# A fourth buffer of probabilities, one buffer for b_2, and a new hand-written order of the steps of a batch

## The chip, the cores and the metric

The kernel runs on one core of a Trainium2 chip. The metric is the device time of one execution in microseconds (us), median of three runs. All data are float32; products that need more than one pass are built from a high and a low part.

## The reference

The input `x` has 16 batches of 512 tokens with 256 features. Two networks read the layer-normed input, and their product is added to `x`:

```python
xn = layernorm(x)
s = talk(xn)              # 16 heads of 16; 512 x 512 logits per head
g = silu(local(xn))       # two layers
out = x + s * g

# talk: rope on q and k, then
logits = einsum('bhij,gh->bgij', q k^T * scale, Wpre)
attn = einsum('bhij,gh->bgij', softmax(logits), Wpost)
out = (attn @ v) @ Wout.T + bout

# local, per layer: shift half of the features by one token,
# q k v = h @ wqkv (8 heads of 64), l2norm of q and k, rotary,
# softmax over a window of 128 tokens and the one before, x += o @ wo,
# layernorm, h @ w1 + b1 -> a, g;  x += (a * gelu(g)) @ w2 + b2
```

## The kernel before, in words

All weights but the four large ones of each layer stay in SBUF. `program()` lays out one list of steps for the whole run: `FIRST_ORDER` for batch 0, `ORDER` for batches 1 to 14, `LAST_ORDER` for batch 15. A step is a name with indices, such as `scores.13`. Each engine has a function for each step that it takes part in, and `Counts.run` calls these in the order of the list. So the list sets the order of each engine's queue by itself; between engines there are only semaphores. An engine that waits in a step holds back all that it has in later steps.

The steps of the talk network, per batch: `expand.c` (POOL, L1561 to L1571) multiplies q by the pre-mixing weights, `part.c` makes the high part (ACT, L1041) and the low part (POOL, L1575), for two tiles of queries at a time. `scores.n` (64 of them) is six matmuls (L759 to L761) into bank S0 or S1 (n even or odd), a row maximum on DVE (L1307), and the exponential on ACT (L1054) into `probs`, which has PB buffers. `mixers.m` (32) takes the reciprocals of the row sums (DVE, L1299) and scales the post-mixing weights (ACT, L1062). `mix.m` is 64 matmul records (L776) on two tiles, 2m and 2m+1, into banks M0 and M1; ACT empties M0 and DVE empties M1 (both L573). `values.c` and `project.t` follow for each eight and sixteen tiles, in M0.

The steps of the local network, per layer l: `qkv.l.t`; on DVE the rotation (L1330) and the squared norms (L1338, L1344), on POOL the power -1/2 (`qkv`, L1586); `join.l.t` adds on DVE (L1357) and scales k on POOL (L1593); `q_turn` and `k_turn` transpose (L835) into F3 and M1. `local_scores.l.u` (8), `weigh.l.u` (POOL, L1601), `p_turn.l.u`, `local_values.l.u` (into M1; DVE empties it, L1416), `out_proj.l.t` (into F3; DVE adds the input, L1430), `half_turn`, `shift_turn`, `h_scale`, `h_turn`, then `up.l.i`, `hide.l.i` and `down.l.t`. The gate of the previous batch is finished in the first third of the next one: `bound`, `sigmoid.t` (DVE reciprocal, L1510), `silu` (POOL, L1623), `gated` (POOL, L1628), `store`. They use `x_mid`, which the DVE part of `out_proj.0.0` overwrites, so that one waits for `gated_done`.

The waits that the change touches, in ACT's `scores`:

```python
before = (n - PB) // 2
if n >= PB:
    act.wait_ge(filled["M1"], now.fill(("mix", before), "M1"))
```

PE may start `scores.n` when ACT has emptied that S bank of tile n-2 and when `part` of n//2 is done. It may start a `mix` when M0 and M1 have been emptied of what they held.

Of the kernel before, what the change touches and what calls it, by code (L numbers as in the profile page):

```python
# [136 lines left out]
weigh.0.6 project.0 weigh.0.7 local_values.0.4 p_turn.0.5 mix.9 p_turn.0.6 local_values.0.5 part.12 scores.21
out_proj.0.2 expand.13 local_values.0.6 p_turn.0.7 scores.22 local_values.0.7 mixers.10 scores.23 out_proj.0.3 mix.10
half_turn.0 mixers.11 part.13 scores.24 expand.14 shift_turn.0 mix.11 scores.25 scores.26 mixers.12 values.2 part.14
h_scale.0 scores.27 mix.12 mixers.13 expand.15 h_turn.0 part.15 scores.28 scores.29 mix.13 expand.16 up.0.0 mixers.14  # L140
# [1597 lines left out]
```

## Time and profile before

| what | us |
|---|---|
| median of 3 runs | 5136.95 (5134.96 to 5141.85) |
| the profiled execution | 5127.82 |
| its span, first to last instruction | 5126.0 |
| PE busy in the span | 4968.1 (97%) |
| DVE busy | 3403.0 (66%) |
| ACT busy | 3111.0 (61%) |
| POOL busy | 2884.7 (56%) |

A busy time is the union of an engine's instructions. The profile lists for each group of instructions the count, the mean duration, and the idle time of the engine just before them with what ended it. PE is the matmul engine, POOL is GpSimd. The page's mean DMA rate is 64 GB/s.

### The profile page before, as it was taken

To read this page: it belongs to the slowest core of one execution; us is meant where nothing else is said; L and a number is where in the kernel's file an instruction comes from. 1 tells how busy PE (TensorE), PEld (TensorE's weight loads), DVE (VectorE), ACT (ScalarE), POOL (GpSimd) and SP (SyncE) were. 2 spreads that over 40 slices of the span, in tenths; PEclk is the share of its full clock that TensorE was granted. 3 is DMA by queue.
4 is the path that set the end of the run, shared out by engine and by line. 5 is a ranking of instruction groups with operands and counts; after the bars stand their busy time and mean duration, and the time that the engine had idled before them with its cause. 6 is when DMAs were issued, how large, how long until landed. Compare 5 with 4: busy or idle time off the path is not lost. (4 is left out here: it accounts for less than half of the span.)

```text
span 5126.0 us, 184535 instructions
## 1 busy us (share of the span) xinstructions
PE 4968.1 (97%) x76184; PEld 4078.3 (80%) x76184; DVE 3403.0 (66%) x8316; ACT 3111.0 (61%) x8075; POOL 2884.7 (56%) x2500
## 2 busy tenths in 40 slices
PE   6999999999999999999999999999999999999998
PEld 5787888878878788788787877878788788878887
DVE  6557676676766667666676666767667676676765
ACT  4566655666655666556665566565566655666655
POOL 4547555465655656555565555655546555465653
PEclk9999999999999999999999999999999999999999
DMA  2312112121111211112111111112112122121111
GB/s 85 119 51 86 46 74 75 42 69 70 54 74 46 74 58 54 74 46 78 54 54 74 66 62 50 64 64 74 54 61 71 46 74 71 45 70 63 57 62 30
DMA packets 61215, 325.84 MB, mean 64 GB/s; under 512 B 6368, under 2 KB 23776, under 8 KB 43488
## 3 DMA queue, kind: packets, MB, share of 16 engines
q1 hardware_dynamic: 49632, 297.26, 15.4%
q0 software_dynamic: 10752, 16.78, 1.7%
q8 instruction: 610, 9.99, 0.8%
q14 instruction: 221, 1.81, 0.1%
HBM read 288.33 MB, written 34.08 MB: 63 GB/s over the span
## 5 line engine op out<-in xcount | busy, mean ns | idle before, releaser
L1575 POOL TENSOR_TENSOR q_lo<-q_mix,q_hi 128x512 fp32r<-128x512 f32 x512 | 662.1, 1293 | 863.0 <-ACT q_hi L1041 862.7
L1054 ACT ACTIVATE probs<-bank_S,neg_max 128x512 f32<-128x512 f32 x1024 | 699.0, 684 | 725.2 <-DVE neg_max L1307 639.1
L759 PE MATMUL bank_S<-k_hi,q_lo 128*128 128x512 f32 x2048 | 879.4, 429 | 35.3 <-POOL q_lo L1575 21.6
L1307 DVE TENSOR_REDUCE neg_max<-bank_S 128x1 f32<-128x512 f32 x1024 | 697.0, 687 | 295.8 <-PE bank_S L761 290.7
L761 PE MATMUL bank_S<-k_hi,q_hi 128*128 128x512 f32 x2048 | 806.3, 394 | 0.0
L760 PE MATMUL bank_S<-k_lo,q_hi 128*128 128x512 f32 x2048 | 805.6, 393 | 0.0
L1570 POOL TENSOR_TENSOR q_mix<-q_rope,w_pre 128x256 f32<-128x256 f32 x1024 | 633.1, 646 | 43.4 <-POOL q_lo L1575 0.9
L776 PEld LDWEIGHTS bank_M<-mixer_n,probs 64*64 64x64 f32 x32768 | 530.5, 135 | 155.9 <-issue 135.8
L776 PE MATMUL bank_M<-mixer_n,probs 64*64 64x64 f32 x32768 | 597.9, 221 | 8.1 <-DVE o_locT_lo L1416 3.4
L1601 POOL TENSOR_TENSOR l_probs<-l_probs,l_inv 128x1024 f32<-128x1024 f32 (+1 forms) x256 | 430.2, 1688 | 273.6 <-DVE l_inv L1410 272.8
L1586 POOL TENSOR_TENSOR inv_norms<-norms_c,minus_half 128x16 f32<-128x16 f32 x128 | 418.1, 3266 | 251.2 <-DVE norms_c L1344 249.2
L1607 POOL TENSOR_TENSOR hidden_lo<-shared,hidden_hi 128x512 fp32r<-128x512 f32 x192 | 246.5, 1300 | 547.0 <-ACT hidden_hi L1185 546.9
L1116 ACT ACTIVATE l_probs<-l_probs,l_least 128x256 f32<-128x256 f32 (+1 forms) x1024 | 480.2, 471 | 104.3 <-DVE l_least L1390 101.9
L759 PEld LDWEIGHTS bank_S<-k_hi,q_lo 128*128 128x128 f32 x2048 | 386.0, 188 | 170.2 <-issue 73.0
L573 DVE COPY mixed<-bank_M 128x512 f32<-128x512 f32 x512 | 352.0, 687 | 190.8 <-PE bank_M L776 187.1
L1041 ACT ACTIVATE q_hi<-q_mix 128x512 fp32r<-128x512 f32 x512 | 321.0, 627 | 250.5 <-POOL q_mix L1570 248.8
L761 PEld LDWEIGHTS bank_S<-k_hi,q_hi 128*128 128x128 f32 x2048 | 386.1, 189 | 89.6 <-issue 0.3
L760 PEld LDWEIGHTS bank_S<-k_lo,q_hi 128*128 128x128 f32 x2048 | 388.1, 190 | 56.0
L1390 DVE CUSTOM_DVE_ANT_0 l_probs<-bank_F,mask,inv_norms 128x256 f32<-128x256 f32 (+1 forms) x1024 | 403.5, 448 | 0.7 <-issue 0.7
L1062 ACT ACTIVATE mixer_n<-mixer,row_inv 128x64 f32<-128x64 f32 x1024 | 300.8, 344 | 112.8 <-DVE row_inv L1299 111.9
L1487 DVE SCALAR_TENSOR_TENSOR shared<-bank_F,b,shared 128x512 f32<-128x512 f32 x192 | 143.6, 748 | 327.7 <-ACT shared L1179 308.0
L1330 DVE TENSOR_TENSOR shared<-bank_F,rot 128x512 f32<-128x512 f32 x512 | 323.6, 684 | 51.9 <-PE bank_F L709 51.2
(157 smaller groups left out, 11372.0 us busy)
## 6 DMA issues: line engine op xcount, KB each, us to landing
w_qkv_hi<-split_qkv SPq DMA_DIRECT2D x30, 1536.0 KB, 9.7
w_qkv_lo<-split_qkv SPq DMA_DIRECT2D x30, 1536.0 KB, 6.4
w_hi<-split SPq DMA_DIRECT2D x30, 1408.0 KB, 6.1
w_lo<-split SPq DMA_DIRECT2D x30, 1408.0 KB, 6.1
w_hi<-split SPq DMA_DIRECT2D x30, 768.0 KB, 5.4
w_lo<-split SPq DMA_DIRECT2D x30, 768.0 KB, 7.2
w_o_hi<-split_o SPq DMA_DIRECT2D x30, 512.0 KB, 3.7
w_o_lo<-split_o SPq DMA_DIRECT2D x30, 512.0 KB, 4.7
```

The lines of the kernel that those rows point to most:

```text
L759: mm(bank[k][:], q_lo[q], k_hi[:, s, :], start=(s == 0), stop=False)
L760: mm(bank[k][:], q_hi[q], k_lo[:, s, :], start=False, stop=False)
L761: last = mm(bank[k][:], q_hi[q], k_hi[:, s, :], start=False, stop=(s == 1))
L776: last = mm(bank[f"M{r}"][keys, at:at + GH * HI], probs[rows, (2 * m + t) % PB, j * P + keys.start:j * P + keys.stop], mixer_n[rows, m % 2 ...
L1054: fn(probs[:, n % PB, :], bank[k][:], ACT.Exp, bias=neg_max[:, n % 2:n % 2 + 1], accum_out=row_sum[:, n % 4:n % 4 + 1]).then_inc(emptied[k ...
L1116: fn(l_probs[:, u % LB, j, lo:], l_probs[:, u % LB, j, lo:], ACT.Exp, scale=-1.0, bias=l_least[:, u % 2, j:j + 1], accum_out=l_sum[:, u % ...
L1307: v.tensor_reduce(neg_max[:, n % 2:n % 2 + 1], bank[k][:], AX.X, ALU.max, negate=True)\
L1390: ins = v.tensor_tensor_reduce(l_probs[:, u % LB, j, lo:], bank[k][:, pair * 2 * P + lo:(pair + 1) * 2 * P], mask[:, lo:], inv_norms[:, t, ...
L1570: g.tensor_tensor(q_mix[:, s].rearrange("p m (i g) -> p (m i) g", g=GH), q[:, :, None].to_broadcast(shape), w_pre[:, None, :].to_broadcast ...
L1575: g.tensor_tensor(q_lo[:, c % QB], q_mix[:], q_hi[:, c % QB].bitcast(F32), ALU.subtract)\
L1586: g.tensor_tensor(inv_norms[:, t, :], norms_c[:], minus_half[:], ALU.pow).then_inc(inv_norm_done, 1)
L1601: g.tensor_tensor(l_probs[:, u % LB, :, lo:], l_probs[:, u % LB, :, lo:], l_inv[:, u % 2, :, None].to_broadcast([P, 4, 2 * P - lo]), ALU.m ...
```

## The change

`PB` goes from 3 to 4, so the exponential of tile n waits for `mix` of (n-4)//2 and not of (n-3)//2. `b_2`, which had one buffer for each layer, filled once, has one for both; it is loaded by a DMA on SP's queue at each `out_proj.l.0`, after a wait for the last use, and POOL waits for it in `half_turn`. `ORDER` is new throughout; the other two orders stay. Of `ORDER` the diff below shows the stretches that are spoken of.

```diff
--- before
+++ after
@@ -28,7 +28,7 @@
 CI = CT * RI
 CHUNKS = TILES // CT
 PAIRS = TILES // 2
-PB = 3
+PB = 4
 GR = 4
 RH = 2
 HI = RI // RH
...
 ORDER = """
-expand.0 part.0 expand.1 qkv.0.0 join.0.0 part.1 scores.0 scores.1 qkv.0.1 scores.2 expand.2 bound q_turn.0.0 mixers.0
-join.0.1 part.2 k_turn.0.0 expand.3 qkv.0.2 q_turn.0.1 k_turn.0.1 scores.3 scores.4 part.3 mix.0 join.0.2 mixers.1
-expand.4 qkv.0.3 part.4 q_turn.0.2 mix.1 scores.5 join.0.3 mixers.2 k_turn.0.2 scores.6 scores.7 expand.5 mix.2
-sigmoid.0 part.5 expand.6 q_turn.0.3 k_turn.0.3 mixers.3 scores.8 part.6 local_scores.0.0 scores.9 mix.3
...
-weigh.0.1 mix.4 weigh.0.2 mixers.5 scores.12 sigmoid.2 expand.8 local_values.0.0 part.8 p_turn.0.1 expand.9 scores.13
-silu mix.5 sigmoid.3 gated p_turn.0.2 local_values.0.1 mixers.6 part.9 local_scores.0.3 scores.14 scores.15
-out_proj.0.0 mix.6 store expand.10 mixers.7 local_scores.0.4 weigh.0.3 scores.16 scores.17 part.10 mix.7 expand.11
...
-up.0.1 hide.0.0 hide.0.1 up.0.2 part.16 up.0.3 hide.0.2 hide.0.3 up.0.4 up.0.5 hide.0.5 hide.0.4 scores.30 expand.17
-mix.14 scores.31 scores.32 mixers.15 down.0.0 down.0.1 down.0.2 down.0.3 part.17 expand.18 part.18 mix.15 x_turn.1
-expand.19 scores.33 qkv.1.0 join.1.0 part.19 qkv.1.1 join.1.1 values.3 q_turn.1.0 k_turn.1.0 qkv.1.2 mixers.16
-q_turn.1.1 k_turn.1.1 scores.34 join.1.2 scores.35 expand.20 mix.16 part.20 qkv.1.3 k_turn.1.2 q_turn.1.2 mixers.17
-scores.36 join.1.3 scores.37 mix.17 q_turn.1.3 scores.38 k_turn.1.3 expand.21 part.21 mixers.18 project.1
...
-local_values.1.7 mixers.26 project.2 expand.29 out_proj.1.3 part.29 expand.30 scores.54 half_turn.1 scores.55 mix.26
-mixers.27 part.30 scores.56 expand.31 shift_turn.1 mix.27 scores.57 scores.58 mixers.28 h_scale.1 values.6 part.31
-scores.59 mix.28 mixers.29 h_turn.1 scores.60 scores.61 mix.29 mixers.30 up.1.0 up.1.1 hide.1.0 scores.62 norm
-hide.1.1 scores.63 mix.30 mixers.31 up.1.2 up.1.3 mix.31 scale hide.1.2 hide.1.3 up.1.4 values.7 x_turn.0 up.1.5
-project.3 hide.1.5 hide.1.4 talk_k talk_q down.1.0 down.1.1 down.1.2 talk_v down.1.3
+expand.0 part.0 expand.1 qkv.0.0 part.1 join.0.0 scores.0 expand.2 scores.1 qkv.0.1 mixers.0 k_turn.0.0 part.2
+join.0.1 q_turn.0.0 scores.2 expand.3 qkv.0.2 part.3 q_turn.0.1 expand.4 k_turn.0.1 scores.3 bound scores.4 join.0.2
+part.4 expand.5 mix.0 qkv.0.3 mixers.1 k_turn.0.2 scores.5 join.0.3 part.5 q_turn.0.2 scores.6 expand.6 mix.1 mixers.2
+scores.7 k_turn.0.3 sigmoid.0 part.6 scores.8 mixers.3 mix.2 expand.7 scores.9 q_turn.0.3 part.7 sigmoid.1 scores.10
+mix.3 mixers.4 local_scores.0.0 scores.11 expand.8 weigh.0.0 values.0 part.8 local_scores.0.1 mixers.5 mix.4
+local_scores.0.2 scores.13 scores.12 p_turn.0.0 weigh.0.1 weigh.0.2 local_scores.0.3 mix.5 scores.14 scores.15
+expand.9 sigmoid.2 local_values.0.0 part.9 mixers.6 mixers.7 p_turn.0.1 expand.10 scores.16 scores.17 mix.6
+local_scores.0.4 sigmoid.3 local_values.0.1 silu weigh.0.3 p_turn.0.2 gated part.10 expand.11 scores.18 scores.19
+mix.7 mixers.8 local_scores.0.5 out_proj.0.0 local_values.0.2 weigh.0.4 values.1 mixers.9 p_turn.0.3 local_scores.0.6
+mix.8 scores.20 scores.21 p_turn.0.4 store weigh.0.5 weigh.0.6 local_values.0.3 part.11 mixers.10 local_scores.0.7
...
+scores.24 mix.10 out_proj.0.3 mix.11 half_turn.0 scores.25 part.14 shift_turn.0 scores.26 expand.15 scores.27 part.15
+values.2 mixers.12 h_scale.0 expand.16 mixers.13 scores.28 scores.29 mix.12 h_turn.0 scores.30 mix.13 mixers.14
+scores.31 mixers.15 up.0.0 up.0.1 part.16 hide.0.0 hide.0.1 mix.14 up.0.2 up.0.3 hide.0.2 hide.0.3 up.0.4 expand.17
+up.0.5 mix.15 hide.0.5 hide.0.4 scores.32 scores.33 values.3 mixers.16 down.0.0 down.0.1 down.0.2 part.17 expand.18
+part.18 expand.19 down.0.3 mix.16 part.19 x_turn.1 scores.34 expand.20 scores.35 part.20 qkv.1.0 mixers.17 join.1.0
+qkv.1.1 expand.21 mix.17 q_turn.1.0 scores.36 scores.37 join.1.1 k_turn.1.0 qkv.1.2 k_turn.1.1 mixers.18 part.21
+join.1.2 scores.38 expand.22 q_turn.1.1 qkv.1.3 mix.18 q_turn.1.2 scores.39 scores.40 join.1.3 part.22 expand.23
+k_turn.1.2 mixers.19 project.1 scores.41 q_turn.1.3 k_turn.1.3 mixers.20 part.23 expand.24 scores.42 local_scores.1.0
...
+p_turn.1.1 mixers.22 mixers.23 weigh.1.3 scores.48 scores.49 mix.22 local_scores.1.4 scores.50 mix.23 p_turn.1.2
...
+local_values.1.7 mixers.26 expand.30 scores.55 mixers.27 out_proj.1.3 mix.26 half_turn.1 mix.27 shift_turn.1 part.30
+scores.56 scores.57 values.6 h_scale.1 mixers.28 scores.58 scores.59 h_turn.1 mix.28 mixers.29 scores.60 scores.61
+norm expand.31 up.1.0 up.1.1 mix.29 hide.1.0 hide.1.1 scale up.1.2 part.31 mixers.30 hide.1.2 up.1.3 mix.30 x_turn.0
+scores.62 scores.63 hide.1.3 mixers.31 up.1.4 up.1.5 mix.31 talk_k hide.1.5 hide.1.4 talk_q values.7 talk_v down.1.0
+down.1.1 down.1.2 down.1.3 project.3
 """
...
         b_1 = [sb(f"b_1{l}", [BLOCKS]) for l in range(LAYERS)]
-        b_2 = [sb(f"b_2{l}", [D]) for l in range(LAYERS)]
+        b_2 = sb("b_2", [D])
...
         opener = sb("opener", [1])
@@ -461,6 +461,7 @@
         w_1_loaded = sem("w_1_loaded", 16 * LAYERS, -16 * LAYERS)
         w_1_lo_loaded = sem("w_1_lo_loaded", 16 * LAYERS, -16 * LAYERS)
         w_2_loaded = sem("w_2_loaded", 32 * LAYERS, -32 * LAYERS)
+        b_2_loaded = sem("b_2_loaded", 16 * LAYERS)
         o_hi_done = sem("o_hi_done", TW * QUADS * LAYERS)
         hidden_hi_done = sem("hidden_hi_done", LAYERS * HC)
         hidden_lo_done = sem("hidden_lo_done", LAYERS * HC)
@@ -515,7 +516,7 @@
         for l in range(LAYERS):
             once += [
                 (scales[l], a["scales"][l]), (b_1[l][:], a["b_1"][l]),
-                (b_2[l][:], a["b_2"][l]), (ln_w[l][:], a["ln_w"][l]),
+                (ln_w[l][:], a["ln_w"][l]),
             ]
         LOADED = 16 * len(once)
         TABLES = 2 + 4 * LAYERS + 2
@@ -641,8 +642,12 @@
                         sp.dma_start(w_1_lo[:].bitcast(F32), split_1[l, 1]).then_inc(w_1_lo_loaded, 16)
 
             def out_proj(step, l, t):
-                if t == 0 and now.first:
-                    spill_o(l)
+                if t == 0:
+                    if now.first:
+                        spill_o(l)
+                    if now.past(l):
+                        sp.wait_ge(mid_b_ready, now.at(mid_b_ready, l))
+                    sp.dma_start(b_2[:], a["b_2"][l]).then_inc(b_2_loaded, 16)
                 if t == TW - 1:
                     sp.wait_ge(filled["F3"], now.fill(step, "F3"))
                     sp.wait_ge(o_spilled, 32 * (l + 1) if now.first else 32 * LAYERS)
@@ -710,6 +715,8 @@
 
             def x_turn(step, l):
                 stream_ready(pe, now, l)
+                if now.b == 1 and not l:
+                    pe.wait_ge(bias_folded, LAYERS)
                 for c in range(KC):
                     if now.was_filled(step, f"F{c}"):
                         pe.wait_ge(emptied[f"F{c}"], now.fill(step, f"F{c}") - 1)
@@ -1609,7 +1616,8 @@
 
             def half_turn(step, l):
                 pool.wait_ge(emptied["F3"], now.fill(("out_proj", l, TW - 1), "F3"))
-                g.tensor_tensor(x_mid_b, x_mid[:], b_2[l][:, None, :].to_broadcast([P, TW, D]), ALU.add)\
+                pool.wait_ge(b_2_loaded, now.at(b_2_loaded, 16 * (l + 1)))
+                g.tensor_tensor(x_mid_b, x_mid[:], b_2[:, None, :].to_broadcast([P, TW, D]), ALU.add)\
                     .then_inc(mid_b_ready, 1)
                 if not l and now.b < B - 1:
```

## Rows read from the trace of the kernel before

**Rows 1.** The page: engines, busy us, share of the span, instructions.
```profile
PE 4968.1 (97%) x76184; PEld 4078.3 (80%) x76184; DVE 3403.0 (66%) x8316; ACT 3111.0 (61%) x8075; POOL 2884.7 (56%) x2500
```

**Rows 2.** The page: busy tenths of PE in 40 slices of the span.
```profile
PE   6999999999999999999999999999999999999998
```

**Rows 3.** Busy by stretch (batches 1 to 14): us, engines with counts, clock, DMA.
```profile
397.30:4800.60 4403.30, 4321.29 (x66585) 3546.26 (x66586) 2955.97 (x7254) 2707.35 (x7056) 2520.33 (x2187) 1.00 0.18 62
```

**Rows 4.** Waits of PE, batches 1 to 14: us in total, times, longest.
```profile
PE bank_M L835 <- POOL shared L1593: 16.8, 28, 1.0
PE bank_S L759 <- POOL q_lo L1575: 16.2, 14, 1.2
PE bank_S L759 <- ACT probs L1054: 12.9, 14, 0.9
PE bank_M L795 <- issue: 10.5, 14, 1.5
PE bank_M L835 <- DVE mixed L573: 5.8, 14, 0.4
PE bank_F L707 <- DVE xT_lo L1263: 4.6, 14, 0.6
PE bank_F L718 <- DVE shared L1487: 3.4, 13, 0.4
PE bank_M L776 <- DVE o_locT_lo L1416: 3.4, 14, 0.2
```

**Rows 5.** PE in order of time, batch 6, around scores.31 and scores.32: start, duration.
```profile
2104.40 0.40 PE L760 MATMUL bank_S<-k_lo,q_hi 128*128 128x512 f32 x1
2104.63 0.40 PE L761 MATMUL bank_S<-k_hi,q_hi 128*128 128x512 f32 x1
2105.95 0.47 PE L759 MATMUL bank_S<-k_hi,q_lo 128*128 128x512 f32 x1 [0.92 <-ACT probs L1054]
```

**Rows 6.** POOL in order of time, the start of batch 6 (qkv.0.0 starts at 1966.26).
```profile
1972.19 3.92 POOL L1586 TENSOR_TENSOR inv_norms<-norms_c,minus_half 128x16 f32<-128x16 f32 x1 [2.25 <-DVE norms_c L1344]
1976.18 1.05 POOL L1593 TENSOR_TENSOR shared<-shared,inv_norms 128x512 f32<-128x512 f32 x1
1977.19 1.27 POOL L1575 TENSOR_TENSOR q_lo<-q_mix,q_hi 128x512 fp32r<-128x512 f32 x1
1979.02 2.90 POOL L1586 TENSOR_TENSOR inv_norms<-norms_c,minus_half 128x16 f32<-128x16 f32 x1 [0.57 <-DVE norms_c L1344]
```

**Rows 7.** DVE in order of time, the same stretch: the addition of join.0.0.
```profile
1972.11 1.23 DVE L1357 TENSOR_TENSOR shared<-shared 128x1024 f32<-128x1024 f32 x1
```

**Rows 8.** PE in order of time, batch 6: mix.10, half_turn.0, scores.24.
```profile
2066.99 1.16 PE L776 MATMUL bank_M<-mixer_n,probs 64*64 64x64 f32 x64
2068.09 0.66 PE L911 MATMUL bank_F<-ident,x_mid 128*128 128x128 f32 x4
2068.50 0.48 PE L759 MATMUL bank_S<-k_hi,q_lo 128*128 128x512 f32 x1
```

**Rows 9.** DVE in order of time: it empties M1 of mix.10.
```profile
2068.32 0.69 DVE L573 COPY mixed<-bank_M 128x512 f32<-128x512 f32 x1 [0.79 <-PE bank_M L776]
```

**Rows 10.** Groups by line, DVE, shapes apart, batch 6: busy, mean ns, idle before.
```profile
L1307 DVE TENSOR_REDUCE neg_max<-bank_S 128x1 f32<-128x512 f32 x64 | 43.5, 687 | 19.9 <-PE bank_S L761 19.6
L1390 DVE CUSTOM_DVE_ANT_0 l_probs<-bank_F,mask,inv_norms 128x256 f32<-128x256 f32 x48 | 20.5, 481 | 0.0
L1510 DVE RECIPROCAL x_mid<-x_mid 128x256 f32<-128x256 f32 x4 | 7.0, 1739 | 0.0
```

**Rows 11.** Groups by line, POOL, shapes apart, batch 6.
```profile
L1601 POOL TENSOR_TENSOR l_probs<-l_probs,l_inv 128x1024 f32<-128x1024 f32 x12 | 22.7, 1898 | 9.9 <-DVE l_inv L1410 9.8
L1623 POOL TENSOR_TENSOR x_mid<-x_mid,x_tok 128x1024 f32<-128x1024 f32 x1 | 2.4, 2412 | 0.7 <-DVE x_mid L1510 0.7
L1628 POOL TENSOR_TENSOR s_tok<-s_tok,x_mid 128x1024 f32<-128x1024 f32 x1 | 2.4, 2397 | 0.1
```

**Rows 12.** DMA issues by line: engine, count, KB each, median us to landing.
```profile
b<-in_b SPq DMA_DIRECT2D x2, 128.0 KB, 4.0
```

More of the change, by code:

```diff
@@ L126 @@
 ORDER = """
-expand.0 part.0 expand.1 qkv.0.0 join.0.0 part.1 scores.0 scores.1 qkv.0.1 scores.2 expand.2 bound q_turn.0.0 mixers.0
-join.0.1 part.2 k_turn.0.0 expand.3 qkv.0.2 q_turn.0.1 k_turn.0.1 scores.3 scores.4 part.3 mix.0 join.0.2 mixers.1
-expand.4 qkv.0.3 part.4 q_turn.0.2 mix.1 scores.5 join.0.3 mixers.2 k_turn.0.2 scores.6 scores.7 expand.5 mix.2
-sigmoid.0 part.5 expand.6 q_turn.0.3 k_turn.0.3 mixers.3 scores.8 part.6 local_scores.0.0 scores.9 mix.3
-local_scores.0.1 weigh.0.0 scores.10 expand.7 mixers.4 values.0 sigmoid.1 part.7 local_scores.0.2 scores.11 p_turn.0.0
@@ L132 @@
-weigh.0.1 mix.4 weigh.0.2 mixers.5 scores.12 sigmoid.2 expand.8 local_values.0.0 part.8 p_turn.0.1 expand.9 scores.13
-silu mix.5 sigmoid.3 gated p_turn.0.2 local_values.0.1 mixers.6 part.9 local_scores.0.3 scores.14 scores.15
-out_proj.0.0 mix.6 store expand.10 mixers.7 local_scores.0.4 weigh.0.3 scores.16 scores.17 part.10 mix.7 expand.11
-local_scores.0.5 scores.18 weigh.0.4 weigh.0.5 p_turn.0.3 local_values.0.2 mixers.8 values.1 local_scores.0.6
-local_values.0.3 p_turn.0.4 part.11 scores.19 scores.20 mix.8 mixers.9 local_scores.0.7 out_proj.0.1 expand.12
@@ L137 @@
[L137 to L140, printed above, removed]
-up.0.1 hide.0.0 hide.0.1 up.0.2 part.16 up.0.3 hide.0.2 hide.0.3 up.0.4 up.0.5 hide.0.5 hide.0.4 scores.30 expand.17
@@ L147 @@
-part.22 mix.19 local_scores.1.2 scores.42 weigh.1.1 weigh.1.2 local_values.1.0 values.4 mixers.20 expand.23
-local_scores.1.3 p_turn.1.1 scores.43 mix.20 scores.44 local_values.1.1 part.23 mixers.21 weigh.1.3 p_turn.1.2
-scores.45 local_scores.1.4 expand.24 mix.21 part.24 mixers.22 scores.46 expand.25 weigh.1.4 out_proj.1.0
-local_values.1.2 p_turn.1.3 part.25 scores.47 mix.22 mixers.23 local_scores.1.5 scores.48 scores.49 mix.23
-local_scores.1.6 weigh.1.5 p_turn.1.4 local_values.1.3 expand.26 mixers.24 values.5 part.26 expand.27 local_scores.1.7
@@ L152 @@
-scores.50 out_proj.1.1 weigh.1.6 mix.24 p_turn.1.5 weigh.1.7 local_values.1.4 scores.51 local_values.1.5 part.27
-p_turn.1.6 mixers.25 scores.52 expand.28 out_proj.1.2 local_values.1.6 p_turn.1.7 part.28 mix.25 scores.53
-local_values.1.7 mixers.26 project.2 expand.29 out_proj.1.3 part.29 expand.30 scores.54 half_turn.1 scores.55 mix.26
-mixers.27 part.30 scores.56 expand.31 shift_turn.1 mix.27 scores.57 scores.58 mixers.28 h_scale.1 values.6 part.31
-scores.59 mix.28 mixers.29 h_turn.1 scores.60 scores.61 mix.29 mixers.30 up.1.0 up.1.1 hide.1.0 scores.62 norm
@@ new lines @@
+mix.7 mixers.8 local_scores.0.5 out_proj.0.0 local_values.0.2 weigh.0.4 values.1 mixers.9 p_turn.0.3 local_scores.0.6
+mix.8 scores.20 scores.21 p_turn.0.4 store weigh.0.5 weigh.0.6 local_values.0.3 part.11 mixers.10 local_scores.0.7
+project.0 out_proj.0.1 local_values.0.4 p_turn.0.5 expand.12 mix.9 p_turn.0.6 local_values.0.5 weigh.0.7 part.12
+scores.22 out_proj.0.2 expand.13 local_values.0.6 p_turn.0.7 scores.23 local_values.0.7 part.13 mixers.11 expand.14
+scores.24 mix.10 out_proj.0.3 mix.11 half_turn.0 scores.25 part.14 shift_turn.0 scores.26 expand.15 scores.27 part.15
@@ new lines @@
+join.1.2 scores.38 expand.22 q_turn.1.1 qkv.1.3 mix.18 q_turn.1.2 scores.39 scores.40 join.1.3 part.22 expand.23
+k_turn.1.2 mixers.19 project.1 scores.41 q_turn.1.3 k_turn.1.3 mixers.20 part.23 expand.24 scores.42 local_scores.1.0
+mix.19 scores.43 local_scores.1.1 values.4 weigh.1.0 part.24 local_scores.1.2 mixers.21 mix.20 scores.45 scores.44
+weigh.1.1 p_turn.1.0 local_scores.1.3 weigh.1.2 mix.21 expand.25 scores.46 scores.47 local_values.1.0 part.25
+p_turn.1.1 mixers.22 mixers.23 weigh.1.3 scores.48 scores.49 mix.22 local_scores.1.4 scores.50 mix.23 p_turn.1.2
@@ new lines @@
+weigh.1.4 local_values.1.1 local_scores.1.5 expand.26 scores.51 out_proj.1.0 weigh.1.5 local_values.1.2 p_turn.1.3
+part.26 mixers.24 values.5 local_values.1.3 p_turn.1.4 mix.24 mixers.25 expand.27 part.27 local_scores.1.6 weigh.1.6
+out_proj.1.1 project.2 local_values.1.4 expand.28 p_turn.1.5 part.28 mix.25 local_scores.1.7 expand.29
+local_values.1.5 p_turn.1.6 weigh.1.7 scores.52 scores.53 out_proj.1.2 part.29 local_values.1.6 p_turn.1.7 scores.54
+local_values.1.7 mixers.26 expand.30 scores.55 mixers.27 out_proj.1.3 mix.26 half_turn.1 mix.27 shift_turn.1 part.30
```

1 line of the change is left out of this document (removed).

## The prediction

> **What bounds the kernel now.** First the page: PE is busy for 97% of the span [rows 1], and in the 40 slices only the first is clearly short [rows 2]. So the only things worth asking are how much PE stands idle, and at which steps. Then the busy table: in batches 1 to 14, all of which run `ORDER`, PE is busy 4321.29 of 4403.30 us [rows 3]. That is 314.5 us a batch with 82.0 / 14 = 5.9 us idle, at a granted clock of 1.00, so no step there pays for a low clock. DVE, ACT and POOL are busy 67%, 61% and 57% of it; they set the end only where PE waits for them. Then the waits of PE [rows 4]: nearly all come 14 or 28 times, with nearly the same length, so they are places in the order and not chance. The change touches no matmul's size or number; it can move only these waits, bring new ones, and change what neighbours what.
>
> A wait costs more than its idle time. scores.32 starts 2105.95 - 2104.63 = 1.32 us after the last matmul of scores.31, where 0.23 is the usual distance, so the 0.92 idle cost 1.09 [rows 5]. I add 0.17 to each wait.
>
> **Waits that go**, per batch:
> - scores.32 waits for ACT to empty S0 (12.9 / 14 = 0.92) [rows 4]. Before, the exponential of scores.30 stands in ACT's queue behind all of up.0 and hide.0. In the new order tiles 28 to 31 are exponentiated ahead of up.0.0, and mix.14 and mix.15 run among the `up` steps; that needs the fourth buffer. Late next is S0 for scores.34, with 14 us of values.3 and down.0 in between. 1.09.
> - k_turn.1.0 and k_turn.1.1 wait for POOL's scaling of k (16.8 / 14 = 1.20 in two waits). Now mix.17 and two scores, some 4 us, stand between qkv.1.1 and k_turn.1.0, and all of qkv.1.2 (4.2 us) before k_turn.1.1. My addition of POOL's work there (power 3.9, expand.21 1.2, join 1.0) has it ready at 169.2 us from the batch's start where PE comes at 169.4. 1.20 + 0.34 = 1.54.
> - k_turn.0.3 waits for DVE to empty M1 after mix.2 (5.8 / 14 = 0.41); now it comes ahead of mix.2. 0.58.
> - qkv.1.0 waits for the low part of x (0.33); two scores instead of one cover it. 0.50.
> - x_turn.0 waits for DVE in F0 and F1 (3.4 / 13 = 0.26); it now follows mix.30. 0.43.
> - mix.5 waits for M1, because local_values.0.0 came just ahead (0.24). Now that comes after. 0.41.
>
> Sum 4.55 us a batch.
>
> **A wait that only moves.** scores.2 waits 1.16 for part.1, which POOL runs behind the power of qkv.0.0 and join.0.0 [rows 4]. The power starts at 1972.19, 5.93 after the batch's start, when DVE has the norms; then 3.92, 1.05 and 1.27 us follow, and part.1 is done at 12.2 [rows 6]. The new order swaps part.1 and join.0.0 and puts k_turn.0.0, which needs join.0.0, ahead of scores.2. The same three instructions end at 12.2 and PE arrives at 11.1 either way. Zero; a gain of 1.0 if the swap shortened it, a loss of 1.0 if expand.2, now ahead of the power of qkv.0.1, pushes join.0.2 (I have 27.0 for it against PE's 27.7) and join.0.3 (33.4 against 33.9) over their edge.
>
> In these rows the power takes 3.92 when it starts beside DVE's addition of two SBUF tiles, and 2.90 later [rows 6, 7]. The Trainium skill, SBUF — State Buffer, section SBUF: two separate sides, says that GpSimd and a DVE operation with two SBUF inputs exclude each other on a shared port for a whole instruction, and whichever starts first holds it. That agrees with POOL's 1.02 lost here; the other half, DVE held up by a running POOL instruction, these rows do not show. By that rule DVE's join.0.1 would stand behind a running power, and k_turn.0.1 with it; the sum would be 21 to 41 us higher, as worked out from rows in the second rival.
>
> **Waits that come**, per batch:
> - mix.27 has only half_turn.1 between it and mix.26. A mix starts at 2066.99, DVE copies M1 from 2068.32 for 0.69, so M1 is free 2.02 after the start [rows 8, 9]. Mix and half_turn take 1.10 + 0.41 = 1.51 on PE [rows 8]. 0.5, and a little for the restart: 0.55. The pair mix.10 and mix.11 has out_proj.0.3 (1.5) between and is clear.
> - scores.58 needs S0, whose maximum stands on DVE behind shift_turn.1 (3.0). My addition has it 0.3 late. 0.3.
> - The knot of sigmoid.3, silu, gated and out_proj.0.0. DVE: local_scores.0.4 (four of 0.48 and small ones, 2.05), sigmoid.3 1.74 [rows 10]; POOL: silu 2.41, weigh.0.3 1.90, gated 2.40 [rows 11]; DVE: out_proj.0.0 0.42, which waits for `gated_done`. With 0.1 a hop, 11.3 us. PE's cover from the end of local_scores.0.4 to the F3 half of p_turn.0.3 is 11.1. Behind the waiting out_proj.0.0 stand DVE's local_values.0.2, weigh.0.4 and local_scores.0.6. Before it, DVE runs behind PE: between scores.12 and scores.17 stand six maxima of 0.69 and sigmoid.2 [rows 10], and local_values.0.1 and mix.7 each find M1 some 0.1 to 0.2 late. 0.8 in all; from 0 (DVE in time) to 3.9 (a rival).
> - About ten other places where my addition leaves under 0.3 us: part.10 before scores.20, weigh.1.7 before p_turn.1.7, the exponential of scores.26, M1 before mix.10 and local_values.1.1. From 0 to 2.5; I take 0.8, a third, as before such places cost mostly nothing.
>
> Sum 2.45 us a batch.
>
> **Edits at no cost.** Scores follow scores 21 times instead of 15, and mixes come after scores 11 times instead of 20; setting the distances of PE's step starts in the trace against both sequences gives 304.0 us a batch without waits for the old and 304.1 for the new, so zero, with 0.6 either way. The waits called issue at `values` (10.5 / 14 = 0.75) [rows 4] have no engine behind them and stay. b_2: one more DMA of 128 KB a layer, 4.0 us to landing [rows 12], issued at out_proj.l.0 some 30 us ahead of half_turn; what SP waits for is a layer old, and the load behind it is due only at local_values.l.7. With no cover it would be 4.0 x 2 = 8 us a batch, on POOL, and only partly on PE. Two loads fewer before the start: 0 to 1 us, taken 0. Batches 0 and 15 keep their orders and gain only looser exponentials: 0 to 2 us, taken 1.
>
> **The sum.** 4.55 - 2.45 = 2.1 us a batch, 29 us in 14, 30 in all. The profiled execution took 5127.8 with a span of 5126.0; 5098 for its like. The median lies 9.1 above the profiled one, so 5107 as a median.
>
> **Rivals.**
> - *Deeper gain* (5065): the new places are all in time and most waits found are gone: 4.55 and the 1.3 of part.1 with it, (4.55 + 0.5) x 14 = 71. For it: three of the four engines are a third idle. Against: mix.27's copy cannot be in time.
> - *The wait moves, nothing is won* (5137): POOL and DVE are late at other steps by as much, 4.5 a batch, because my additions leave no room for contention. One such mechanism: DVE's join.0.1, due while POOL runs the power of qkv.0.1 (2.90 [rows 6]), is held back by it for half of it or all, 1.5 to 2.9 us a batch, which alone turns 5107 into 5128 to 5148. The rows so far show only POOL giving way. (The Trainium skill, SBUF — State Buffer, section SBUF: two separate sides, has both sides giving way.)
> - *The knot closes* (5155, slower): one mechanism. sigmoid.3, silu and gated hold DVE at out_proj.0.0 and PE at p_turn.0.3. It costs one for one beyond 11.1 us; it cancels the gain from 2.1 us more than I have, and with DVE 3.5 late the price is (3.5 - 2.1) x 14 = 19 above 5137. For: DVE's queue is full there. Against: it is 67% busy over the batch and DVE catches up at every PE step without work for it.
> - *The change doesn't bite*: with b_2's load late, half_turn would wait. 30 us of cover against 4: 2 in 100.
>
> **Numbers.** Near the forecast 0.45, deeper gain 0.22, nothing won 0.17, knot 0.13, other 0.03. About 0.2% (10 us) is what a measurement of this kernel can tell from no change. Faster by more: 0.43 + 0.22 + 0.05 of the third case = 0.70; within: 0.13; slower: 0.17. Range 5060 to 5148; around the likeliest alone 5088 to 5125.
>
> **What would show it.** In the waits of PE after: L759 on ACT probs (12.9) and L835 on DVE mixed gone; L835 on POOL shared still at 14 to 18, now once a batch at k_turn.0.0, and L759 on POOL q_lo near nothing; a new row L776 on DVE mixed of 4 to 8; DVE idle before L1430 on POOL s_tok. Batches 1 to 14 at 312.4 us each, idle 3.5 to 4.5. It is wrong if PE's idle is unchanged, or if idle falls and the batch doesn't.

## The result: 0.24% slower

The changed kernel takes 5148.05 us (median; 5137.79 to 5157.77) and the kernel before, run beside it on the same chip, 5134.96 (5127.53 to 5141.85). The ratio is 1.0024, 95% interval 1.0016 to 1.0032. The forecast was 5107, faster; the range's upper end, 5148, is just missed by the median, and the sign is wrong. The profiled executions are a little apart from their medians (before 5127.8, after 5154.1), so differences between these two traces come to 26 us where the medians differ by 13.

### The profile page after: what moved, and what is told of

Same layout as the page of the kernel before. It is cut to its first block and busy times, and to the rows that moved or that the text cites. A ratio compares the mean times of both kernels' runs of the same rounds, so it can differ in the third digit from the quotient of the medians.

```text
span 5152.0 us, 184596 instructions
## 1 busy us (share of the span) xinstructions
PE 4962.2 (96%) x76184; PEld 4108.2 (80%) x76184; DVE 3415.7 (66%) x8316; ACT 3127.4 (61%) x8075; POOL 2878.2 (56%) x2500
## 3 DMA queue, kind: packets, MB, share of 16 engines
q8 instruction: 610, 9.99, 0.8%
## 5 line engine op out<-in xcount | busy, mean ns | idle before, releaser
L1582 POOL TENSOR_TENSOR q_lo<-q_mix,q_hi 128x512 fp32r<-128x512 f32 x512 | 672.7, 1314 | 748.5 <-ACT q_hi L1048 748.4
L766 PE MATMUL bank_S<-k_hi,q_lo 128*128 128x512 f32 x2048 | 875.0, 427 | 19.2 <-ACT probs L1061 11.1
L768 PE MATMUL bank_S<-k_hi,q_hi 128*128 128x512 f32 x2048 | 808.4, 395 | 0.0
L783 PEld LDWEIGHTS bank_M<-mixer_n,probs 64*64 64x64 f32 x32768 | 542.5, 135 | 170.2 <-issue 139.3
L1577 POOL TENSOR_TENSOR q_mix<-q_rope,w_pre 128x256 f32<-128x256 f32 x1024 | 621.2, 628 | 47.4 <-POOL q_lo L1582 0.9
L783 PE MATMUL bank_M<-mixer_n,probs 64*64 64x64 f32 x32768 | 604.7, 221 | 34.3 <-issue 24.5
L1593 POOL TENSOR_TENSOR inv_norms<-norms_c,minus_half 128x16 f32<-128x16 f32 x128 | 391.4, 3058 | 188.3 <-DVE norms_c L1351 184.6
L766 PEld LDWEIGHTS bank_S<-k_hi,q_lo 128*128 128x128 f32 x2048 | 388.2, 190 | 129.7 <-issue 54.3
L768 PEld LDWEIGHTS bank_S<-k_hi,q_hi 128*128 128x128 f32 x2048 | 387.7, 189 | 89.0
L1614 POOL TENSOR_TENSOR hidden_lo<-shared,hidden_hi 128x512 fp32r<-128x512 f32 x192 | 260.4, 1373 | 353.7 <-ACT hidden_hi L1192 353.7
L574 ACT COPY mixed<-bank_M 128x512 f32<-128x512 f32 x512 | 296.6, 579 | 181.0 <-PE bank_M L783 179.5
```

The source lines that it names most:

```text
L574: copy(to, bank[k][:].rearrange("p (t c i) -> p t c i", t=2, i=HI)).then_inc(emptied[k], 1)
L766: mm(bank[k][:], q_lo[q], k_hi[:, s, :], start=(s == 0), stop=False)
L768: last = mm(bank[k][:], q_hi[q], k_hi[:, s, :], start=False, stop=(s == 1))
L783: last = mm(bank[f"M{r}"][keys, at:at + GH * HI], probs[rows, (2 * m + t) % PB, j * P + keys.start:j * P + keys.stop], mixer_n[rows, m % 2 ...
L1577: g.tensor_tensor(q_mix[:, s].rearrange("p m (i g) -> p (m i) g", g=GH), q[:, :, None].to_broadcast(shape), w_pre[:, None, :].to_broadcast ...
L1582: g.tensor_tensor(q_lo[:, c % QB], q_mix[:], q_hi[:, c % QB].bitcast(F32), ALU.subtract)\
```

## The profile after

The span, PE's part of the page and its slices, then the busy table of batches 1 to 14 (the stretch of [rows 3]; columns as there). Lines of the new kernel stand 7 lower than the old ones: `scores` L766 to L768, `mix` L783, `values` L802, the turns of k L842, `local_values` L894.

```profile
span 5152.0 us, 184596 instructions
PE 4962.2 (96%) x76184; PEld 4108.2 (80%) x76184; DVE 3415.7 (66%) x8316; ACT 3127.4 (61%) x8075; POOL 2878.2 (56%) x2500
PE   6999999999999999999999999999999999999998
...
q8 instruction: 610, 9.99, 0.8%
```

```profile
399.27:4826.47 4427.20, 4311.74 (x66584) 3572.40 (x66585) 2970.90 (x7254) 2723.46 (x7057) 2514.47 (x2188) 1.00 0.18 63
```

A batch takes 316.2 us instead of 314.5 [rows 3], and PE stands idle for 115.5 us instead of 82.0. PE's waits in the same stretch, to be set against [rows 4]:

```profile
PE bank_M L783 <- issue: 23.9, 24, 2.4
PE bank_M L802 <- issue: 23.4, 22, 3.2
PE bank_M L842 <- POOL shared L1600: 17.4, 28, 1.1
PE bank_M L802 <- ACT mixed L574: 12.3, 14, 0.9
PE bank_S L766 <- ACT probs L1061: 10.5, 42, 0.4
PE bank_M L894 <- DVE mixed L574: 9.2, 28, 0.3
PE bank_M L783 <- DVE mixed L574: 5.8, 14, 0.4
PE bank_F L863 <- DVE l_least L1397: 3.5, 8, 0.5
PE bank_F L863 <- issue: 2.5, 3, 1.1
```

The engine waits changed places as meant. The two top rows are new in kind: 46 waits called issue (the profile found nothing that released them), up to 3.2 us long and not in every batch. Before, that name had 10.5 us at `values` [rows 4], a row at `local_scores` that [rows 4] leave out, and 0.2 us at `mix`:

```profile
PE bank_F L856 <- issue: 4.7, 15, 0.7
```

The longest one, in PE's timeline (start, duration, line and operation, in brackets the idle time before):

```profile
1454.31 0.90 PE L802 MATMUL bank_M<-mixed,v_heads 128*32 128x64 f32 x51
1458.45 0.48 PE L802 MATMUL bank_M<-mixed,v_heads 128*32 128x64 f32 x9 [3.24 <-issue]
1458.86 0.80 PE L766 MATMUL bank_S<-k_hi,q_lo 128*128 128x512 f32 x1
1459.45 0.63 PE L767 MATMUL bank_S<-k_lo,q_hi 128*128 128x512 f32 x1
```

PE stops in the middle of `values`, between two matmuls of one loop that read the same tiles; nothing can have become ready there but the instruction itself. Behind it the matmuls of scores take 0.63 us instead of 0.39. The table of windows has the reason (PE busy, PEld, DVE, ACT, POOL, granted clock, DMA share, GB/s):

```profile
1450.00:1458.40 8.40, 5.21 (x136) 4.15 (x135) 7.04 (x26) 3.38 (x8) 5.72 (x9) 1.00 0.51 197
1458.40:1461.90 3.50, 3.45 (x17) 2.66 (x17) 0.08 (x1) 1.33 (x5) 1.00 (x2) 0.52 0.02 5
1461.90:1470.00 8.10, 8.06 (x157) 6.36 (x156) 4.86 (x9) 4.03 (x10) 0.00 (x0) 1.00 0.01 3
```

After the wait TensorE runs for 3.4 us at the lower of its two clock levels (0.52 of 2.4 GHz, that is 1.2 GHz). That happens six times in batches 1 to 14, for 3.4 us five times and 6.8 us once, each time at an issue wait of 1.5 to 3.2 us; before, it never happens in these batches. Not every such wait does it: 11 waits are 1.5 us or longer, and behind two of 2.4 and 2.0 us, among others, the clock stays up. At half speed these 23.8 us cost up to 11.9 us beside the waits.

**What runs out.** In the table of DMA queues, between 1454 and 1459, one packet is an instruction block:

```profile
q0 software_dynamic: 27, 0.08, 4.1%
q1 hardware_dynamic: 6, 0.02, 1.4%
q8 instruction: 1, 0.02, 1.2%
```

Queue q8 has 610 packets and 9.99 MB in the whole run, 16 KB each; one holds 256 instructions, as experiment 3 shows. PE has 2 x 76184 records, 595 blocks. Then I took each issue wait above 0.4 us in batches 1 to 14 and counted PE's records, loads and matmuls together, up to it, adding 240 a batch for instructions that leave no record (2 x 76184 + 16 x 240 = 156,208 = 610.2 blocks, the number of packets; that 240 is my fit). Modulo 256 the 45 waits of the new kernel lie at 187 to 196, and the 18 of the old one at 186 to 192. So PE waits at the border of a block. At these waits a fetch takes 0.9 to 1.4 us of packet time, and the wait ends 1.2 to 1.6 us after the fetch has ended. The Trainium skill, Runtime: NRT & Kernel Launch, section Instruction fetch mechanics, says that each engine's instructions come in 16 KiB blocks of 256 by a DMA queue of its own, which agrees, and that crossing a border is mostly hidden because instructions are dispatched more slowly than they are fetched. This trace disagrees for PE: 3.24 us at one border.

`mix` uses up 128 instructions in 1.1 us and `values` 256 in 1.9 us, while `scores` takes 1.5 us over 12. At the two dense steps a block lasts 2 to 4 us with what lies about them. The new order puts dense steps nearer each other: from values.0 to local_scores.0.2 416 records in 4.1 us where nothing is fetched late, mix.26 and mix.27 with one turn between, mix.10 and mix.11 with one out_proj (they start 2.7 us apart). By step the issue waits are mix.27 7.0, mix.11 6.8, values.2 6.2, values.3 5.5, mix.4 4.5, mix.20 4.4, values.6 4.0, values.0 3.7, values.4 3.5; before, only `values` and `local_scores` have more than 0.3 us.

PE's time per batch, worked out for each trace from all its idle times (rest is what is not idle; "issue" is the profile's name, and experiment 8 shows that it can hide an engine):

| kernel | batch | issue | engines | rest |
|---|---|---|---|---|
| before | 314.52 | 1.22 | 4.66 | 308.63 |
| after | 316.23 | 4.01 | 4.27 | 307.95 |
| old order | 314.45 | 1.37 | 4.60 | 308.48 |
| b_2 once | 315.62 | 3.67 | 4.29 | 307.66 |
| shifted | 316.25 | 4.09 | 4.24 | 307.93 |
| spaced, seven edits | 314.55 | 3.04 | 3.30 | 308.21 |
| spaced, six edits (second run) | 314.36 | 3.30 | 2.73 | 308.33 |
| spaced more | 318.46 | 4.50 | 5.70 | 308.26 |
| six edits and mix.15 | 314.15 | 2.55 | 3.55 | 308.05 |

## The experiments

**1. Everything but the order.** The changed kernel with the `ORDER` of before.

```diff
-expand.0 part.0 expand.1 qkv.0.0 part.1 join.0.0 scores.0 expand.2 scores.1 qkv.0.1 ...
+expand.0 part.0 expand.1 qkv.0.0 join.0.0 part.1 scores.0 scores.1 qkv.0.1 scores.2 ...
```

> The changed kernel with the old ORDER: four buffers of probabilities and b_2 in one buffer loaded per layer stay, only the order of steps goes back. Theory A (the new order thins out PE's supply of instructions: it puts mix, values and mix closer together, and the waits called issue, 55 us in batches 1 to 14 after against 16 before, are waits for instructions): as the kernel before, 5130 to 5140, ratio 0.999 to 1.001, issue waits at mix and values back to 10 to 16 us, no fall of the clock in batches 1 to 14. Theory B (the 30 further loads of b_2, in packets of 1 KB, hold up the fetching of instructions): 5145 to 5155, ratio 1.002 to 1.004, issue waits of 40 us or more. Theory C (PB alone does something): any other time.

Measured: 5131.91 us, ratio 0.9997 [0.9988, 1.0006]. Issue waits are back:

```profile
PE bank_M L802 <- issue: 10.1, 17, 1.0
PE bank_F L863 <- issue: 4.5, 12, 1.0
...
PE bank_M L783 <- issue: 1.1, 4, 0.4
```

At `mix` and `values` they sum to 11 us, within the 10 to 16 expected, and the clock does not fall in batches 1 to 14. The order alone makes the kernel slower; the fourth buffer and b_2's loads cost nothing that can be measured.

**2. The new order, b_2 loaded in the first batch only** (layer 0 of the later batches then adds the bias of layer 1).

```diff
-                    if now.past(l):
-                        sp.wait_ge(mid_b_ready, now.at(mid_b_ready, l))
-                    sp.dma_start(b_2[:], a["b_2"][l]).then_inc(b_2_loaded, 16)
+                    if now.first:
+                        if now.past(l):
+                            sp.wait_ge(mid_b_ready, now.at(mid_b_ready, l))
+                        sp.dma_start(b_2[:], a["b_2"][l]).then_inc(b_2_loaded, 16)
...
-                pool.wait_ge(b_2_loaded, now.at(b_2_loaded, 16 * (l + 1)))
+                if now.first:
+                    pool.wait_ge(b_2_loaded, now.at(b_2_loaded, 16 * (l + 1)))
```

> The changed kernel, but b_2 is loaded in batch 0 alone; from batch 1 on both layers use the b_2 of layer 1, so 30 loads of 128 KB are left out and the bias of layer 0 is another one. Theory A (instruction supply, by the order): no change against the changed kernel, ratio to before 1.001 to 1.004, issue waits 40 to 70 us. Theory B (the loads of b_2): ratio 0.999 or lower, issue waits under 25 us.

Measured: 5148.81 us, ratio 1.0027 [1.0016, 1.0039], with the issue waits at the same steps:

```profile
PE bank_M L784 <- issue: 23.9, 22, 2.4
PE bank_M L803 <- issue: 18.0, 18, 1.9
```

b_2's loads do not hold the instruction blocks up. Whether other loads do was not tried. The trace of the changed kernel speaks for it in part: all seven waits of 2 us or more have 160 to 380 GB/s of other transfers from 4 us before the wait to its end, where the mean of the stretch is 63, and the packet of their block starts 0.4 us before PE stops at the earliest. But of the 22 waits of 0.4 us or more with under 5 GB/s around them the longest is still 1.7 us. One window of either kind:

```profile
650.80:657.20 6.40, 3.68 (x97) 3.13 (x97) 1.87 (x4) 3.05 (x9) 2.35 (x1) 0.92 0.94 377
4390.90:4396.70 5.80, 3.25 (x124) 2.44 (x123) 2.39 (x13) 4.52 (x21) 2.25 (x3) 1.00 0.01 3
```

**3 and 4. Half as many instructions in `mix`, in either order.** A mix's four 64x64 tiles become two of 64x128, so 32 matmuls and 32 loads instead of 64 and 64, with the same products. It is a slower mix: what counts is the two orders against each other.

```diff
-                            for half in range(2):
-                                keys = slice(half * (P // 2), (half + 1) * (P // 2))
-                                last = mm(bank[f"M{r}"][keys, at:at + GH * HI],
-                                          probs[rows, (2 * m + t) % PB, j * P + keys.start:j * P + keys.stop],
+                            last = mm(bank[f"M{r}"][:, at:at + GH * HI],
+                                      probs[rows, (2 * m + t) % PB, j * P:(j + 1) * P],
```

> The changed kernel with each mix in 32 matmul records instead of 64: one matmul on 64 rows x 128 keys in place of two on 64 x 64, same result. It takes 2048 records of matmul and weight load from each batch of some 9750. Theory A (instruction supply): issue waits fall from 55 us to under 20, the clock does not fall in batches 1 to 14, and if a mix itself takes no longer than 1.09 us the ratio to before is 0.989 to 0.996 (40 us of waits, 8 of clock, off 5148: 5080 to 5115). Theory B (loads of b_2) or a rival by which the issue waits have to do with bank M and not with the number of instructions: they stay at 40 us or more. If two 64x128 tiles run less side by side than four 64x64, mix takes up to twice as long: +1.1 x 512 = 560 us, and the issue waits still tell the theories apart.

> The kernel before with each mix in 32 matmul records instead of 64, as in the run before this. Theory A: its 16 us of issue waits in batches 1 to 14 fall to under 6; if the mix takes as long as now the ratio is 0.994 to 0.999 (5105 to 5130). The new order is then ahead of the old by what my account of waits between engines gave, 1 to 2 us a batch. If the waits are no matter of instruction supply: ratio 1.000 and the same waits.

Measured: 5509.27 us with the new order (ratio 1.0735 [1.072, 1.075]) and 5542.16 with the old (1.0797 [1.0782, 1.0812]). From the page and the waits (400 to 4850 us, some 13 batches of this length) of the new order, then of the old:

```profile
q8 instruction: 482, 7.90, 0.6%
...
PE bank_M L800 <- issue: 4.1, 6, 1.4
PE bank_F L861 <- issue: 2.0, 2, 1.1
PE bank_M L781 <- issue: 0.8, 3, 0.4
```

```profile
PE bank_M L793 <- issue: 3.9, 4, 1.3
PE bank_F L854 <- issue: 2.9, 9, 0.9
```

128 packets fewer are 32,768 instructions at 256 each, just what was left out (512 mixes with 64 fewer), so q8 is PE's supply. Over all of batches 1 to 14 the issue waits of the new order fall from 55 us to 8, as many as the old order has. For the old order under 6 were expected, so its part of the forecast missed by a little. The clock, which was not expected to fall, fell twice for 3.4 us with the new order, behind waits of only about 1 us. A mix takes 1.93 us from its start to the next step's instead of 1.09, which is why both kernels are slower. Now the new order is 33 us (0.6%) faster than the old. That is the sign and about the size of the forecast's 30, but not its mechanism term by term: over the whole run PE idles 118 us with the new order and 129 with the old, so only 11 of the 33 are waits; and mixes that take 0.84 us longer give the other engines more time in both.

**5. The borders moved by half a block.** 64 transposes at the start, before anything else on PE (64 matmuls and 64 loads).

```diff
+            for _ in range(64):
+                turn(bank["S0"][:, 0:P], ident[:], ident[:])
```

> The changed kernel with 64 transposes (128 records of PE and its weight load) ahead of the first step, where PE stands idle for 30 us anyway. They shift each later instruction of PE by half of a block of 256 against the blocks in which its instructions are fetched. Theory A (each issue wait is at a block's border and is long where the border falls into dense steps): in the same batch the issue waits stand at other steps than in the changed kernel, those between engines stay at the same steps with the same lengths to 0.1 us; the sum of issue waits in batches 1 to 14 is again 35 to 75 us, the time within 10 us of the changed kernel. Theory D (the waits called issue come from something in the steps themselves, a bank or a DMA due then): the same steps of the same batches wait as long as before.

Measured: 5140.2 us, ratio 1.001 [1.0001, 1.0019].

```profile
PE bank_M L785 <- issue: 27.7, 28, 2.5
PE bank_M L804 <- issue: 17.2, 19, 2.2
```

The sum stays (4.09 a batch), but of 54 issue waits above 0.25 us only 2 fall in the same batch and step as one of the 51 of the changed kernel. Counted as before, from the first record, the 45 above 0.4 us again lie at one place of a block, 192 to 200. So the waits go with the borders and not with the data, and the steps only decide how much a border costs. The clock again fell six times, elsewhere. The median is 8 us lower than that of the unshifted kernel, and the two traces put the difference in batch 0, since the later batches take the same time. Batch 1 begins at 383.0 us instead of 399.3: scores.0 starts 3 us earlier behind the transposes, the granted clock from 120 to 180 us is 0.94 instead of 0.89, and an issue wait of 3.3 us near 201 us is not there. What each of these is worth was not tried.

**6. Dense steps apart.** Seven small edits of the new order: six put a `scores` step between two dense steps, and one puts mix.19 ahead of local_scores.1.0. The third also moves scores.26 ahead of part.14, which the expectation does not name:

```diff
-mix.4 local_scores.0.2 scores.13 scores.12
+scores.12 mix.4 local_scores.0.2 scores.13
-local_scores.0.6 mix.8 scores.20 scores.21
+local_scores.0.6 scores.20 mix.8 scores.21
-mix.11 half_turn.0 scores.25 part.14 shift_turn.0 scores.26
+scores.25 mix.11 half_turn.0 scores.26 part.14 shift_turn.0
-mix.20 scores.45 scores.44
+scores.44 mix.20 scores.45
-half_turn.1 mix.27 shift_turn.1 part.30 scores.56
+half_turn.1 scores.56 mix.27 shift_turn.1 part.30
-mix.24 mixers.25 ... weigh.1.7 scores.52 scores.53
+scores.52 mix.24 mixers.25 ... weigh.1.7 scores.53
-scores.42 local_scores.1.0 mix.19
+scores.42 mix.19 local_scores.1.0
```

> The changed kernel with seven edits of ORDER, nothing else: one scores step is put between the dense steps at six places (scores.12 before mix.4, scores.44 before mix.20, scores.20 before mix.8, scores.52 before mix.24, scores.56 between mix.26 and mix.27, scores.25 between mix.10 and mix.11), and mix.19 comes ahead of local_scores.1.0. Theory A (instruction supply, dense neighbours): issue waits in batches 1 to 14 fall from 55 us to 20 to 40, and the two waits between engines that the edits aim at (L783 on DVE mixed 5.8, L802 on ACT mixed 12.3) go; ratio to before 0.993 to 0.999, 5100 to 5130. Theory E (the issue waits are chance, set by how the borders fall, and density does not matter): issue waits stay at 45 us or more, and only the 18 us of the other two waits come off: 5128 to 5138.

Measured: 5133.52 us, ratio 0.9996 [0.9987, 1.0005]; 15 us less than the changed kernel, and not to be told from the kernel before.

```profile
PE bank_M L802 <- issue: 26.4, 23, 2.2
PE bank_F L938 <- issue: 4.3, 5, 0.9
PE bank_M L783 <- issue: 2.7, 4, 0.9
```

At `mix` the issue waits fall from 23.9 to 2.7, at `values` they do not (now values.6, 10.2 in nine batches). The waits of mix.27 for DVE and of values.4 for ACT are gone too, so the gain is not of the supply alone: issue 0.97 a batch less, engines 0.97 less, and the rest 0.26 more. The issue waits sum to 40 us, the upper end of what theory A allows and below theory E; the time lies above A's 5100 to 5130 and within E's range. So spacing the dense steps does thin the waits out, and wins less time than A had it.

**7. The same without the edit at mix.24**, run twice.

```diff
-p_turn.1.4 scores.52 mix.24 mixers.25 ... weigh.1.7 scores.53
+p_turn.1.4 mix.24 mixers.25 ... weigh.1.7 scores.52 scores.53
```

> The new order with six of the seven edits: scores.52 goes back behind weigh.1.7. In the kernel with all seven, out_proj.1.2 waited for pT from ScalarE in each of the 14 batches (7.3 us), which it did not with scores.52 behind weigh.1.7, and mix.24 had no wait called issue to begin with. Theory (two costs that add: waits for instructions at dense places, and waits for engines): the 7.3 us go, the sum of issue waits stays at about 40 us in batches 1 to 14, and the time is about 7 us under the kernel with seven edits, 5126, against 5135 for the kernel before (ratio 0.998). Rival (a wait taken away only moves to the next dense place): issue waits rise by about as much, 5131 to 5135, ratio 0.9995.

> The kernel with six spacing edits once more, unchanged, since its ratio (0.9987, 0.9978 to 0.9996) is close to what can be told from no change. If it is really faster than the kernel before, the ratio lies again between 0.998 and 0.9995; if the first comparison was luck, it lies at 0.9995 to 1.0005 with an interval that holds 1.

Measured: 5128.15 us, ratio 0.9987 [0.9978, 0.9996], and again 5126.81, 0.9986 [0.9977, 0.9995]. The waits of the second run:

```profile
PE bank_M L802 <- issue: 24.3, 25, 2.2
PE bank_M L842 <- POOL shared L1600: 17.5, 28, 1.1
PE bank_M L894 <- DVE mixed L574: 9.2, 28, 0.3
PE bank_M L783 <- issue: 5.7, 9, 1.4
PE bank_S L766 <- ACT probs L1061: 5.4, 14, 0.4
```

The wait for pT is gone (engines 2.73 a batch instead of 3.30), while the issue waits rise from 40 us to 48 in the first run and 44 in the second: a part of what was won came back, as the rival has it, and both medians lie nearer the theory's 5126 than the rival's 5131. This version is some 20 us faster than the changed kernel. It is 0.14% faster than the kernel before, which is less than the 0.2% that I named as the bound, but both intervals leave 1 out. Its issue waits are still 2.1 us a batch above the old order's.

**8. Three more steps moved**: values.6 behind scores.58, mix.15 ahead of up.0.5, h_turn.0 ahead of mix.12.

```diff
-scores.57 values.6 h_scale.1 mixers.28 scores.58 scores.59
+scores.57 h_scale.1 mixers.28 scores.58 values.6 scores.59
-expand.17 up.0.5 mix.15
+mix.15 expand.17 up.0.5
-scores.29 mix.12 h_turn.0 scores.30
+scores.29 h_turn.0 mix.12 scores.30
```

> As the kernel with six edits, with three more steps moved by one or two places: values.6 behind scores.58 (it held 10.2 us of issue waits in nine batches, right behind mix.27 and scores.57), mix.15 ahead of up.0.5 (values.3 behind scores.33 held 5.1), and h_turn.0 ahead of mix.12 (mix.12 waited 5.6 us for ScalarE's mixer_n). Theory: what is spaced out loses its waits: issue waits fall from about 40 to about 25 us, mix.12's 5.6 go, and the time is about 5108 (ratio 0.995). Rival: every block of instructions that is fetched late is met by some step, and moving steps only chooses which; the sum stays at 40, and the time is 5120 to 5127 (0.997 to 0.998).

Measured: 5184.7 us, ratio 1.0099 [1.0086, 1.0113]. Both theories missed it.

```profile
PE bank_M L783 <- DVE mixed L574: 21.3, 14, 1.5
PE bank_F L938 <- issue: 21.1, 24, 1.1
PE bank_S L766 <- ACT probs L1061: 20.2, 28, 1.1
...
PE bank_M L783 <- issue: 15.5, 23, 1.5
PE bank_F L712 <- POOL hidden_lo L1614: 10.3, 14, 0.7
```

h_turn.0 ahead of mix.12 makes mix.13 find its bank unread in every batch and scores.30 its probabilities late (21.3 and 14.9 us). The waits called issue went from values.6 (8.9 us before these moves, now 1.2) to h_turn.1, h_turn.0 and mix.28 (11.3, 9.8 and 9.2). That looks like the rival, but it is mostly not the supply. Of the 72 issue waits above 0.15 us, 34 with 26.5 us lie away from a block's border, all at the first matmul of these three steps, at mix.28 in every batch; in the changed kernel none of 57 does. Each of these starts 0.10 us after another engine's instruction that the step needs: DVE's last line of `h_scale` (L1463) or ACT's copy of M0 after `values` (L1083). In batch 6, where DVE ends at 2256.93:

```profile
2255.57 1.36 DVE L1463 TENSOR_SCALAR shared<-bank_F,mean_var,rstd 128x128 f32<-128x128 f32 x4
...
2257.04 1.06 PE L938 MATMUL bank_F<-ident,shared 128*128 128x128 f32 x8 [0.81 <-issue]
```

So these are waits for engines that the profile leaves without a name. The waits at borders sum to 35 us, against 44 and 40 in the two runs of experiment 7. The row L938 of experiment 6 is of the same kind for 3.4 of its 4.3 us.

**9. Only mix.15 of these**, on top of the six edits.

> The kernel with six spacing edits and mix.15 moved ahead of up.0.5. In the kernel with more moves, this one took the issue waits of values.3 away (5.2 us to none), and the others (h_turn.0 ahead of mix.12, values.6 behind scores.58) brought 21.3 us at mix.13 and 20 us at h_turn.1 and mix.28. Theory (a dense place can be thinned where no engine's due time stands in the way): values.3's 5.2 us go and nothing comes, 5123 (ratio 0.9976). Rival (the blocks fetched late only meet another step): the sum of issue waits stays at 47 and the time at 5128 (0.9987). Second rival: mix.15 earlier waits for mixers or DVE as mix.13 did, and the time is 5135 to 5145.

Measured: 5130.41 us, ratio 0.9995 [0.9986, 1.0004]: not to be told from the six edits. values.3's issue waits (5.2) are gone and the sum of issue waits fell from 48 and 44 to 33, but up.0.5 now stands behind a mix of 1.1 us, and down.0.0 now waits for the hidden part in each batch (`PE bank_F L712 <- POOL hidden_lo L1614`, 10.3 again). The supply can be thinned out, at the price of a wait of another kind.

## Why the prediction was wrong

**The step that failed** is the sentence "The waits called issue at `values` (10.5 / 14 = 0.75) [rows 4] have no engine behind them and stay", put among the edits at no cost. What they waited for was PE's next block of instructions, and on that an order has an effect. The waits called issue rose by 2.8 us a batch, and the lower clock behind the longest took up to 0.85 more: 39 us and up to 12. The row misled by its count: 14 times in 14 batches, as the waits for engines. By step they are values.0 twice, values.2 five times, values.4 twice, values.5 four times and values.6 once, and the mean of 0.75 against a longest of 1.5 shows that they don't have one length. The 4.7 us at `local_scores` were not in the account either; all issue waits before came to 1.22 us a batch.

**Waits that go.** All six went. The row of scores.32 (12.9) has no successor there, no turn of layer 1 waits for POOL, and x_turn.0, qkv.1.0, k_turn.0.3 for DVE, and mix.5 have none.

**The wait that moves** did so exactly: L842 on POOL shared has 17.4 (14 to 18 were foretold), 15.2 of it at k_turn.0.0 and 2.2 at k_turn.0.3. The SBUF rival of a join held up by the running power found nothing here: k_turn.0.1 doesn't wait. In the whole trace 78 of DVE's 128 additions (L1364) start 0.3 to 2.6 us into a running power and take 1.20 to 1.22 us, and the power beside them 2.90. Only a power that starts beside a running addition is longer, 3.8 to 3.9. So only POOL gives way here, as in the rows before.

**Waits that come.** mix.27 0.64 in distance against 0.55. The knot did not close: p_turn.0.3 has one wait in 14 batches, 0.6 for an instruction block, though DVE stands up to 2.3 us at out_proj.0.0, whose first instruction waits for `gated` (`DVE x_mid L1437 <- issue: 27.3, 14, 2.3`; the profile doesn't name POOL there, the code does). scores.58 has no row, nor have the five places named among the "about ten other". Not foreseen: values.4, 0.9 a batch, because ACT's copy of the bank that it needs stands behind the four exponentials of local_scores.1.0; local_values.1.5, 0.33; scores.50, 0.4; and three smaller ones. local_values.0.1 waits 0.33, where 0.1 to 0.2 was seen. The waits that go were worth 3.35 us of idle time a batch, as read, and those that come 2.95. Engines take 4.27 a batch instead of 4.66: 0.4 better, where the two sums made it 2.1 with the restarts. So this term was mis-sized too: the sum gave seven waits a restart as they go, 1.2 us, and as good as none to those that come, of which there are as many.

**Neighbours.** "So zero, with 0.6 either way": PE's rest fell by 0.68 a batch although the lower clock is in it, so by up to 1.5. That was not in the sum. In the pair of experiments 3 and 4, where the supply hardly counts, the new order is ahead by 2.3 us a batch, and 1.65 of it is this rest. So the pair comes near the forecast's 30 us by another road, which is luck and no support for the sum. Which neighbours do it was not tried and stays open. The 304.0 us a batch without waits is 4.6 less than the 308.6 that the trace of before leaves, so of that working only the difference of the two orders could be used.

**The sum**, per batch: issue +2.79, engines -0.39, rest -0.68, together +1.71; times 14 is 24 of the 26 us between the traces. Without issue and clock it would be 1.1 to 1.9 faster, where 2.1 was forecast. b_2 and PB at nothing were right.

**The rivals.** None was it. (The deeper gain names 4.55 and 1.3 but adds 4.55 and 0.5; 5065 follows from the latter.) "Nothing won", the nearest at 5137, had POOL and DVE late elsewhere; what came was slower by a cause that no rival named.
